# Turning a tenth block per tile by DMA, two blocks to a transfer, in a masked attention kernel

## The reference

```
h = maximum(layernorm(x), 0)                    # x: 8192 x 128
scores = leaky_relu(h @ ks.T, 0.2)              # ks: 8192 x 128
scores = where(adj > 0, scores, -9e15)
out = x + softmax(scores, axis=1) @ ks
```

## Time and profile before

| | before |
|---|---|
| median of 3 runs | 1596.42 us (1595.24 to 1597.04) |
| profiled execution, own time | 1591.91 us |
| its span | 1590.0 us |
| granted PE clock | 0.998 of full speed |
| busy PE / DVE / ACT / POOL | 1560.3 / 1418.5 / 1342.3 / 1329.5 us |
| transposing DMAs, blocks turned | 572 |

### The profile page before, as it was taken

How to read it: one execution, slowest core, us unless ns; L and a number is a source line. 1 busy time by engine, 2 the same in 40 slices (tenths; PEclk the granted TensorE clock), 3 DMA queues, 4 the chain that set the end, 5 groups by cost and what they waited for, 6 DMA issues and landing times.

```text
span 1590.0 us, 37555 instructions
## 1 busy us (share of the span) xinstructions
PE 1560.3 (98%) x13202; PEld 1156.2 (73%) x13202; DVE 1418.5 (89%) x2527; ACT 1342.3 (84%) x2008; POOL 1329.5 (84%) x1348
## 2 busy tenths in 40 slices
PE   5899999999999999999999999999999999999998
PEld 3577777777777777777777777777777777777777
DVE  7998998999899899889889989998998998999896
ACT  6788888888888888888888888888888888888886
POOL 3688888888888888888888888888888888888885
PEclk9999999999999999999999999999999999999999
DMA  9999999999999999999999999999999999999995
GB/s 315 282 276 274 293 282 279 277 284 277 280 283 274 283 280 263 275 281 279 275 267 298 273 280 279 292 270 271 295 263 289 268 279 285 282 282 281 269 282 94
DMA packets 701626, 437.67 MB, mean 275 GB/s; under 512 B 629760, under 2 KB 629760, under 8 KB 701440
## 3 DMA queue, kind: packets, MB, share of 16 engines
q1 hardware_dynamic: 701440, 435.27, 112.7%
HBM read 276.82 MB, written 4.19 MB: 177 GB/s over the span
## 4 chain that ended last, share of the span: by engine, by line
PE 94%; DMA 1%; POOL 1%; DVE 1%; ACT 1%; issue 0%; POOLq 0%; DVEq 0%; ACTq 0%
PE ps_out L434 27%; PE ps_out L435 14%; PE ps_scores L408 13%; PE ps_scores L409 13%; PE ps_scores L407 13%; PE ps_T L418 12%; DMA keys_in<-keys_in 1%; PE ps_out L433 0%; PE ps_out L384 0%; ACT scores L505 0%; POOL keys_in L348 0%; POOL keys_in L346 0%; DVE scores L628 0%; PE ps_out L432 0%; ACT scores L496 0%
## 5 line engine op out<-in xcount | busy, mean ns | idle before, releaser
L348 POOL TENSOR_TENSOR keys_in<-scores,keys_in 128x512 f16<-128x512 f32 x572 | 720.6, 1260 | 46.1
L628 DVE CUSTOM_DVE_ANT_0 scores<-ps_scores,mask,minus_scale 128x1024 f32<-128x1024 f32 x512 | 653.9, 1277 | 16.1 <-PE ps_scores L409 1.2
L496 ACT ACTIVATE scores<-scores 128x1024 f32<-128x1024 f32 x512 | 538.0, 1051 | 77.9 <-DVE pair_min L628 77.9
L346 POOL CAST keys_in<-scores 128x512 f16<-128x512 f32 x572 | 460.0, 804 | 162.6 <-ACT scores L505 159.5
L505 ACT ACTIVATE scores<-scores,neg_max 128x1024 f32<-128x1024 f32 x512 | 583.4, 1140 | 0.1
L434 PE MATMUL ps_out<-keys,keys_in 128*128 128x256 f16 x2225 | 428.6, 273 | 3.1 <-DMA keys_in<-keys_in 3.1
L643 DVE TENSOR_TENSOR probsT_lo<-ps_T,probsT_hi 128x512 f16<-128x512 f32 x452 | 310.6, 687 | 123.6 <-ACT probsT_hi L513 114.9
L407 PE MATMUL ps_scores<-keysT_hi,hT_hi 128*128 128x512 f16 x1024 | 389.0, 380 | 13.9 <-DVE keysT_lo L599 9.7
L435 PE MATMUL ps_out<-keys,keys_in 128*128 128x128 f16 x2225 | 398.0, 219 | 0.0
L513 ACT ACTIVATE probsT_hi<-ps_T 128x512 f16<-128x512 f32 x447 | 264.5, 592 | 155.5 <-PE ps_T L418 152.1
L408 PE MATMUL ps_scores<-keysT_lo,hT_hi 128*128 128x512 f16 x1024 | 389.0, 380 | 0.0
(11 more groups left out here) (57 smaller groups left out, 825.7 us busy)
## 6 DMA issues: line engine op xcount, KB each, us to landing
adj_in<-in_adj_dram SPq DMA_DIRECT2D x512, 512.0 KB, 5.3
keys_in<-keys_in SPq DMA_TRANSPOSE x572, 5.6
x_in<-in_x_dram SPq DMA_DIRECT2D x16, 256.0 KB, 4.0
keys_in<-in_L_gnn_ks_dram SPq DMA_DIRECT2D x8, 512.0 KB, 7.1
out_dram<-out_tile SPq DMA_DIRECT2D x16, 256.0 KB, 4.1
keys<-keysT_hi SPq DMA_TRANSPOSE x8, 4.7
keys<-keysT_lo SPq DMA_TRANSPOSE x8, 4.6
```

The costliest lines, as they stand in the source:

```text
L346: nc.gpsimd.tensor_copy(half[:, 0:BLOCK], probs(t, b)).then_inc(half_hi_ready, 1)
L348: nc.gpsimd.tensor_tensor(half[:, BLOCK:2 * BLOCK], probs(t, b), half[:, 0:BLOCK], ALU.subtract) \
L496: nc.scalar.activation(s, s, ACT.Prelu, alpha=1.0 / SLOPE).then_inc(leaky_ready, 1)
L628: nc.vector.tensor_tensor_reduce(out=score_pair(q, p), in0=ps_scores[:, slots, :].rearrange("p s k -> p (s k)"), in1=mask[:, (p // 2) % 2, ...
```

## The change

Block 4 goes over from `BY_PE` to `BY_DMA`, in 63 tiles, so ten blocks a tile are turned by DMA (1, 3, 4, 5, 7, 9, 11, 12, 13, 15). In the last tile block 8 goes over. One transposing DMA now turns two blocks that follow each other in this list; the pairs are (1,3), (4,5), (7,9), (11,12) and (13,15). It is issued where the second of the two was issued, and one semaphore tells that both have landed. The cast that makes the high half of blocks 4 and 12 is done by ACT (`cast_half`), three slots behind the scores, and POOL waits for it before it subtracts. `turned` has 10 slots in place of 8. PE multiplies a turned block one slot later (`ADD_LAG` 11). The transposes of x move from slot 12 to 13, `split_h` from 13 to 14, and `finish` from 10 to 11.

```diff
-    D_SLOTS = 8
+    D_SLOTS = 10
-    ADD_LAG = 10
-
-    BY_DMA = tuple(b for b in range(BLOCKS) if b % 2 == 1 or b in (12,))
+    ADD_LAG = 11
+
+    BY_DMA = tuple(b for b in range(BLOCKS) if b % 2 == 1 or b in (4, 12))
+    CAST_BY_ACT = (4, 12)
-    LAST_BY_DMA = (1, 3, 5, 7, 9)
-    LAST_BY_DVE = (0, 2, 4, 6, 8)
+    LAST_BY_DMA = (1, 3, 5, 7, 8, 9)
+    LAST_BY_DVE = (0, 2, 4, 6)
...
+        def wait_halves(engine, n):
+
+            if n >= R_SLOTS:
+                m = n - R_SLOTS
+                engine.wait_ge(turned_in[m % D_SLOTS // 2], 16 * (m // D_SLOTS + 1))
...
-            def turn(t, b):
+            def turn_two(t, b):
+
                 n = nth_dma(t, b)
                 sp.wait_ge(half_lo_ready, n + 1)
...
-                sp.dma_start(turned[:, n % D_SLOTS, :, :], halves[:, n % R_SLOTS, :], transpose=True) \
-                    .then_inc(turned_in[n % D_SLOTS], 16)
+                to, of = (n - 1) % D_SLOTS, (n - 1) % R_SLOTS
+                sp.dma_start(turned[:, to:to + 2, :, :].rearrange("p s k c -> p (s k) c"),
+                             halves[:, of:of + 2, :].rearrange("p s k -> p (s k)"), transpose=True) \
+                    .then_inc(turned_in[to // 2], 16)
...
-                        if turning:
-                            turn(*turning)
+                        if turning and nth_dma(*turning) % 2 == 1:
+                            turn_two(*turning)
...
+                if b in cast_by_act(t):
+                    pool.wait_ge(act_half_ready, len(CAST_BY_ACT) * t + CAST_BY_ACT.index(b) + 1)
                 else:
...
+            def cast_half(t, b):
+                n = nth_dma(t, b)
+                act.wait_ge(probs_ready, t * PAIRS + b // 2 + 1)
+                wait_halves(act, n)
+                nc.scalar.activation(halves[:, n % R_SLOTS, 0:BLOCK], probs(t, b), ACT.Copy).then_inc(act_half_ready, 1)
...
+                    cast = behind(i, j, LO_LAG, cast_by_act, this, prev)
+                    if cast:
+                        cast_half(*cast)
                     split = behind(i, j, T_LAG, by_pe, this, prev)
```

More of the change, by code:

```diff
@@ L157, in gat_kernel @@
         half_hi_ready = sem("half_hi_ready")
+        act_half_ready = sem("act_half_ready")
         half_lo_ready = sem("half_lo_ready")
-        turned_in = [sem(f"turned_in{s}") for s in range(D_SLOTS)]
+        turned_in = [sem(f"turned_in{s}") for s in range(D_SLOTS // 2)]
         out_done = sem("out_done")
@@ L198, in nth_dma, with cast_by_act @@
             return sum(len(by_dma(s)) for s in range(t)) + sum(c < b for c in by_dma(t))
+        def cast_by_act(t):
+            return CAST_BY_ACT if t < TILES - 1 else ()
+        def wait_halves(engine, n):
+            if n >= R_SLOTS:
+                m = n - R_SLOTS
+                engine.wait_ge(turned_in[m % D_SLOTS // 2], 16 * (m // D_SLOTS + 1))
+            else:
+                engine.wait_ge(keysT_done, BLOCKS)
+                engine.wait_ge(scale_steps, PAIRS)
         def wait_hi(engine, t, b):
@@ L338, in split_half @@
                 pool.wait_ge(probs_ready, t * PAIRS + b // 2 + 1)
-                if n >= R_SLOTS:
-                    m = n - R_SLOTS
-                    pool.wait_ge(turned_in[m % D_SLOTS], 16 * (m // D_SLOTS + 1))
-                else:
[L343 to L347, removed]
+                half = halves[:, n % R_SLOTS, :]
+                if b in cast_by_act(t):
+                    pool.wait_ge(act_half_ready, len(CAST_BY_ACT) * t + CAST_BY_ACT.index(b) + 1)
+                else:
+                    wait_halves(pool, n)
+                    nc.gpsimd.tensor_copy(half[:, 0:BLOCK], probs(t, b)).then_inc(half_hi_ready, 1)
+                    cast = sum(len(by_dma(s)) - len(cast_by_act(s)) for s in range(t)) \
+                        + sum(c <= b and c not in cast_by_act(t) for c in by_dma(t))
+                    pool.wait_ge(half_hi_ready, cast)
                 nc.gpsimd.tensor_tensor(half[:, BLOCK:2 * BLOCK], probs(t, b), half[:, 0:BLOCK], ALU.subtract) \
@@ L449, in output_turned @@
                 n = nth_dma(t, b)
-                pe.wait_ge(turned_in[n % D_SLOTS], 16 * (n // D_SLOTS + 1))
+                pe.wait_ge(turned_in[n % D_SLOTS // 2], 16 * (n // D_SLOTS + 1))
                 for k in range(PER_BLOCK):
@@ L475, in step @@
                         output_turned(*added)
-                    if j == 12 and ahead:
+                    if j == 13 and ahead:
                         transpose_h(i + 2, odd)
@@ L702, in step @@
                             minimum(i + 1)
-                    if ahead and j == 13:
+                    if ahead and j == 14:
                         split_h(i + 2, odd)
@@ L714, in step @@
                         weigh(i - 1)
-                    if prev and j == 10:
+                    if prev and j == 11:
                         finish(i - 1, 1 - odd)
```

## The result

The changed kernel takes 1742.6 us in the median of 4 runs (1738.0 to 1743.9), against 1596.1 us for the kernel before. The ratio is 1.091 (95% interval 1.089 to 1.093), so it is 146.6 us slower where 21 us less had been forecast.

The account below looks back on a forecast made before the run. PE was taken to bound the kernel: 1591.9 us less 28.0 for transposes plus 7 for late pairs gives 1571; the median lies 4.5 above, so 1575 us. The 8-in-10 range was 1566 to 1610 us.

Parts of the forecast that it names:

- What bounds the kernel: PE, busy 1560.3 of 1590.0 us with 94% of the chain, sets the tile time, 24.09 us before the change.
- the gain of 28 us: On PE, transposes of 64 blocks go away at 0.437 us each, saving 28.0 us.
- for as long as nothing else becomes late: Condition under which work taken from PE was worth its whole length.
- What the others get: Added load elsewhere: ACT 0.48 us a tile, hidden; POOL 0.46 more, to 89%; SP 5 turning issues in place of 9.
- No engine but PE becomes full: Claim after summing loads of ACT, DVE and POOL; SP's two-block issue was taken as 2.5 us.
- What can be late: Turned pairs: (7,9) has least room, 5.8 us against 5.0 needed; late now and then, 0.12 us a tile, 7 us.
- In this place SP has had some 2.5 us without an issue: Before pair (7,9), a pause on SP was claimed, so landing was taken as 5.0 us, nearer the empty end.
- The first: Rival: pair (7,9) is late in every tile, PE waits 0.9 us a tile, 1624 us; range 1600 to 1630, chance 0.24.
- The rule of the Trainium skill: 261 GB/s for a transposing DMA, so ten blocks take 10.0 us a tile; added weight to the late-pair rival.
- The third rival: Score cadence hurts DVE: a missed mask addition costs 0.5 us a tile, 1599 us; chance 0.14 shared with the second.

Follow-up runs that it names:

- e2: The changed kernel with all ten casts on POOL and none on ACT, pairs kept: 1737.7 us, 1.088 to the kernel before.
- e5: The kernel before plus a tenth transposing DMA of one block a tile, into a spare slot that nobody reads: 1707.3 us, 1.066.
- e4: The changed kernel with each adjacency load after the first eight cut to half its columns: 1609.1 us, 1.008 to the kernel before.
- e8: The kernel before with each adjacency load after the first eight cut to half its columns: 1588.8 us, 0.992.
- e6: The kernel before plus a plain, not transposing, copy of 256 KB a tile into a spare slot: 1611.9 us, 1.007.
- e1: The changed kernel with one block to a transposing DMA, ten a tile, in place of pairs: 1701.5 us, 1.066 to the kernel before.
- e7: The version of e1 with adjacency loads issued from ACT in place of SP: 2222.1 us, 1.388 to the kernel before.

## Why the prediction was wrong

- *What bounds the kernel.* PE did hold the chain, and its price was right: 388 blocks, and four transposes that still take 858.23 - 857.79 = 0.44 us. A tile before was put at 24.09 us and takes 24.12. No run shows the gain of 28 us itself, since in none with fewer transposes did PE alone set the pace. The sentence "for as long as nothing else becomes late" carried it all.
- *What the others get.* ACT's cast took 0.61 us, near the 0.6 of the forecast, and moving it changes nothing (e2). POOL's extra wait for it is the longest in the profile and costs nothing either: POOL waits since everybody waits. The step that failed is the last one there, "No engine but PE becomes full", with SP's load taken from the size of single issues. It never adds up a tile of SP or of the DMA engines. The stream was all but full before the change: 22 us of pauses in 1000, and a further turn of 1.7 us that nobody waits for makes a tile 1.7 us longer (e5).
- *What can be late.* "In this place SP has had some 2.5 us without an issue": it had none, and came 0.9 us late. I took 5.0 us from ready to landed, and measured 7.6 + 0.9 = 8.5 in the tile shown. POOL's part was right: I had the cast of block 4 and the two blocks after it, then 7 and 9, ending 10.2 us after the cast, and in the tile shown it went from 850.7 to 860.2, 9.5 us. The time for two blocks with nothing ahead, forecast at 4.3, was 4.3.
- *The rivals.* The first had the right place and sign, and its price of 0.9 us a tile was that of a latency. The loss is mainly a rate: a full stream makes each tile longer by one more turn (1.7 us), and the 0.44 that PE no longer needs is not seen at all. The pairs' late start, the step that this rival did price, comes on top with 0.6. I had its evidence in hand, issues above 1.75 us and a share of 1.14, and weighed it as a chance, 0.24, where SP's pauses summed over many tiles would have settled it. The rule of the Trainium skill on the rate of transposing DMAs (DMA: Bandwidth & Descriptors, "Latency and other measured facts") spoke for this side. No run gives its 261 GB/s for turned bytes alone, and the page has that figure for a non-contiguous middle dimension. By the packet records a turned byte takes the engines about twice the time of a loaded one. The third rival, DVE's cadence, is not what was lost here: PE's waits for the mask addition are not among the long ones. Its sign does show in e4, once the stream has room.
- The range ended at 1610, since I bounded the wait by landing times and then left out the upper half of the first rival. A landing time bounds a delay that is waited out once a tile; it doesn't bound what a full resource costs.

## What to carry to other kernels

Before work is moved to a queue, look whether the queue has gaps. Here the sign was a stream whose issues followed each other almost without a pause (22 us in 1000) and took longer than their floor (1.75 us for 1.23), while the landing times still left its users slack. The slack only showed that it wasn't yet overfull. An unused extra transfer (e5) is a cheap test of that, and so is the kernel with its loads halved (e8).

## What was not expected of the hardware

- A transposing DMA of 256 KB cost 1.7 us a tile in this mixture, and a plain copy of the same bytes 0.2 (e5, e6: 106.5 and 11.1 us over 64 tiles). By the packets the engines spend 1.7 and 0.8 us on them.
- Loads on a second queue beside the turns brought the rate from 269 to 206 GB/s (e1 against e7). Why is open.
- The mask on DVE grew from 1.27 to 1.65 us in the mean between e8 and e4, with the same loads, as more masks lay beside a subtraction on POOL. The cause wasn't isolated.
- PE's clock. After a wait of 3.9 us the granted clock fell to half, from 2.4 to 1.2 GHz, though PE was busy again by then. The wait, in 810 to 818.5 us of the changed kernel, and the windows around it:

```profile
PE ps_out L451 <- DMA keys_in<-keys_in: 3.9, 1, 3.9
```

```profile
812.00:818.00 6.00, 2.07 (x17) 1.41 (x16) 1.73 (x3) 3.62 (x6) 3.28 (x5) 1.00 1.08 275
818.20:821.40 3.20, 3.20 (x16) 2.19 (x14) 3.16 (x3) 1.03 (x2) 2.15 (x3) 0.50 1.15 199
822.00:828.00 6.00, 6.00 (x55) 4.42 (x53) 4.91 (x12) 4.88 (x8) 1.47 (x2) 1.00 1.08 298
```

PE was busy 2.07 of 6 us at full clock, then 3.2 of 3.2 at half. At half clock it got through 16 matmuls in 3.2 us, at full clock through 55 in 6. The mean clock of the run is 0.989 where it was 0.998, so this long wait cost a little more than its own length.
